# Order of the work inside a turn: VectorE's cosine product, ScalarE's copies and its squares change places in a six-layer attention kernel

## The reference

```
def attn_layer(x, Wqkv, qs, ksc, Wo):
    qkv = x @ Wqkv
    q, k, v = jnp.split(qkv, 3, -1)          # 16 heads of 64
    q = l2norm(q) * qs
    k = l2norm(k) * ksc
    q = q * cos * scale + rotate_half(q) * sin * scale
    k = k * cos * inv + rotate_half(k) * sin * inv
    out = local_attention(q, k, v)           # windows of 32 rows: own window and the one before
    return out @ Wo
...
for i in range(DEPTH):                       # DEPTH = 6
    x = attn_layer(shift_tokens(x), ...) + x
    x = ffn_layer(shift_tokens(x), ...) + x  # layer norm, x @ W1, a * gelu(gate), @ W2
```

## Time and profile before

| | |
|---|---|
| median of 3 runs | 2216.33 us |
| the profiled execution | 2233.99 us, span 2232.2 us |
| TensorE busy | 1985.9 us, 89% |
| VectorE busy | 1626.6 us, 73% |
| GpSimd busy | 1375.4 us, 62% |
| ScalarE busy | 1295.5 us, 58% |
| mean granted TensorE clock | 0.933 of full speed |

### The profile page before, as it was taken

One profiled execution on the slowest core, in us unless ns is written; L12 is line 12 of the kernel. 1 busy time (PEld: TensorE's weight loads), 2 busy tenths in 40 slices (PEclk: granted clock), 3 DMA queues, 4 the chain that ended last, 5 costly groups with the idle time before them and its releaser, 6 DMA issues.

```text
span 2232.2 us, 74626 instructions
## 1 busy us (share of the span) xinstructions
PE 1985.9 (89%) x33032; PEld 1350.5 (61%) x33032; DVE 1626.6 (73%) x1657; ACT 1295.5 (58%) x1547; POOL 1375.4 (62%) x1401
## 2 busy tenths in 40 slices
PE   2678998679999999999999899998999999999986
PEld 1234444357766676666766666666766766676664
DVE  4546564289886888777877788788778976888753
ACT  1145556556765766666566666665666665766642
POOL 1000000399977787679687867787777877887720
PEclk7589999889999999999999899999999999999998
DMA  2410110023332223322223222233222332222221
GB/s 86 122 43 33 33 53 12 26 55 73 71 83 70 64 60 80 82 72 65 57 65 83 74 71 66 69 83 83 60 71 61 78 85 69 68 61 61 63 64 43
DMA packets 132866, 146.28 MB, mean 66 GB/s; under 512 B 60856, under 2 KB 75452, under 8 KB 131776
## 3 DMA queue, kind: packets, MB, share of 16 engines
q1 hardware_dynamic: 132544, 141.51, 25.2%
HBM read 30.51 MB, written 5.44 MB: 16 GB/s over the span
## 4 chain that ended last, share of the span: by engine, by line
DVE 33%; PE 25%; POOL 11%; SPq 10%; issue 9%; ACT 9%; DMA 2%; DVEq 0%; POOLq 0%; ACTq 0%
DVE arena L736 8%; SPq L1266 7%; DVE ss L728 4%; POOL arena L1110 4%; DVE arena L777 4%; DVE arena L767 3%; PE banks L408 3%; DVE mx_t L763 3%; PE banks L575 3%; PE banks L480 3%; DVE arena L639 3%; PE banks L391 2%; POOL arena L1118 2%; ACT arena L995 2%; PE banks L370 2%
## 5 line engine op out<-in xcount | busy, mean ns | idle before, releaser
L1110 POOL TENSOR_TENSOR arena<-arena,tab_sl 128x512 f32<-128x512 f32 x384 | 546.3, 1454 | 37.0 <-ACT arena L931 30.4
L1118 POOL TENSOR_TENSOR arena<-arena 128x1024 f32<-128x1024 f32 x192 | 491.5, 2581 | 0.0
L736 DVE TENSOR_TENSOR arena<-arena,rn 128x1024 f32<-128x1024 f32 x192 | 355.2, 1891 | 79.7 <-POOL rn L1086 79.7
L960 ACT ACTIVATE arena<-arena 128x1024 f32<-128x1024 f32 x96 | 101.5, 1058 | 534.2 <-DVE arena L767 534.2
L471 PE MATMUL banks<-w_qkv,arena 128*128 128x512 f32 x768 | 356.6, 607 | 7.4 <-ACT arena L923 5.5
L538 PE MATMUL banks<-arena 64*64 64x32 f32 x12288 | 252.1, 226 | 42.7 <-DVE arena L767 41.8
L480 PE MATMUL banks<-ident,arena 128*128 128x128 f32 x1536 | 231.7, 307 | 50.2 <-DVE arena L777 32.5
L538 PEld LDWEIGHTS banks<-arena 64*64 64x64 f32 x12288 | 241.0, 139 | 57.4 <-DVE arena L767 48.0
L639 DVE TENSOR_REDUCE arena<-banks 128x1 f32<-128x1024 f32 (+7 forms) x176 | 175.2, 1027 | 124.3 <-PE banks L372 124.1
L880 ACT ACTIVATE arena<-banks 128x1024 f32<-128x1024 f32 (+4 forms) x176 | 150.1, 870 | 153.5 <-PE banks L393 139.3
L480 PEld LDWEIGHTS banks<-ident,arena 128*128 128x128 f32 x1536 | 194.6, 158 | 70.9 <-DVE arena L777 49.8
(11 more groups left out here) (112 smaller groups left out, 3159.2 us busy)
## 6 DMA issues: line engine op xcount, KB each, us to landing
arena<-arena SPq DMA_DIRECT2D x1512, 64.0 KB, 2.0
w_qkv<-Wqkv SPq DMA_DIRECT2D x6, 1024.0 KB, 5.6
arena<-parts_dram SPq DMA_DIRECT2D x96, 48.0 KB
arena<-parts_dram SPq DMA_DIRECT2D x32, 144.0 KB
parts_dram<-arena SPq DMA_DIRECT2D x4, 768.0 KB, 3.3
w_o<-Wo SPq DMA_DIRECT2D x6, 512.0 KB
w_qkv<-Wqkv SPq DMA_DIRECT2D x6, 512.0 KB, 4.2
arena<-X SPq DMA_DIRECT2D x24, 128.0 KB
```

Source lines behind the costliest of these rows:

```text
L736: e.tensor_tensor(to, to, rn[n // 2 % 2][:, n % 2, HEADS * m:HEADS * (m + 1)].unsqueeze(2).to_broadcast([P, HEADS, HEAD_DIM]), ALU.mult).t ...
L1110: e.tensor_tensor(qk_sw[:, m, :].rearrange("p (h d) -> p h d", d=HEAD_DIM)[:, :, d:d + HALF], raw[:, m, :].rearrange("p (h d) -> p h d", d ...
L1118: e.tensor_tensor(to, to, qk_sw[:, m, :], ALU.add).then_inc(S["rs"], 1)
```

## The change

In VectorE's turn `rotate(s)` moves ahead of `norms(s-1)`. In ScalarE's turn `project(s)`, which now only copies, moves ahead of `exponents(s-4)`; the two squares become a function `squares(s)` of their own, between `values(s-2)` and `weights(s-4)`. No instruction is added or removed, and TensorE's, GpSimd's and the DMA queue's programs are the same.

```
 VectorE
                 if 0 <= s - 4 < n_tiles:
                     subtract(s - 4)
+                if s < n_tiles:
+                    rotate(s)
                 if 0 <= s - 1 < n_tiles:
                     norms(s - 1)
-                if s < n_tiles:
-                    rotate(s)
...
 ScalarE
                     e.copy(raw[:, m, :], banks[:, pair_of["proj", n, m], :]).then_inc(S["raw"], 1)
+
+            def squares(n):
+                raw = qk_raw[n % 2]
                 w.wait_ge(S["ss_sum"], n)
...
+                if s < n_tiles:
+                    project(s)
                 if 0 <= s - 4 < n_tiles:
                     exponents(s - 4)
-                if s < n_tiles:
-                    project(s)
...
                 if 0 <= s - 2 < n_tiles:
                     values(s - 2)
+                if s < n_tiles:
+                    squares(s)
                 if 0 <= s - 4 < n_tiles:
                     weights(s - 4)
```

## The result

The change is slower: 2244.36 us against 2216.15 us (medians of 4 runs each), ratio 1.0113, interval 1.0077 to 1.0149 (the two medians alone give 1.0127). A second set of runs of the same change gave 1.0081, 1.0057 to 1.0104. The predicted +0.95% lies between the two ratios. Two sets of one kernel can so differ by 0.3%, and a smaller difference between two kernels says little.

What follows compares the result with a forecast made beforehand. TensorE, 94% busy from 1100 to 2180 us, bounds the kernel through its waits and speed. -4 + 8 + 0 + 21 - 6 + 2 = +21 us: 2233.99 to 2255, or 2237 from the median (+0.95%); range +12 to +32 us, chance 0.48.

Steps and rivals of the forecast that it cites:

- The waits for 777 go and come back at 519: TensorE's 32.5 us of waits at line 480 for cosine products mostly move to line 519, for normalised weights; -4 us.
- a rival: Faster: waits for 777 go for good, slow matmuls could become fewer; -32.5 us, up to 2184, or 2200; chance 0.22.
- Norms later: Sum of squares 2.2 us later delays GpSimd's rn and the subtraction before the k=3 gather; 16 x 0.5 = +8 us.
- The k=3 turn and the squares: Gather to gather from k=3 grows by 1.0 us, through late normalise and squares ahead of the GELUs; 21 groups, +21 us.
- the two chains: In k=3, one over normalise, one over squares and GELUs; both put the next gather 21 us after this one.
- Scale and GpSimd: VectorE's scale runs beside GpSimd's products instead of additions; k=1 gains up to 0.7 us, k=2 can lose it; 0 booked.
- The extra 7 us: If each half of scale in k=1 lost to one GpSimd product, the sum would be about 7 us higher; left out.
- A layer's change: Five times GpSimd waits for the last cosine product before making tables; it comes earlier, half of 2.2 us counted; -6 us.
- Run-in: Turns 4 to 9, without feed-forward: the norms' chain gets longer in three pairs of turns; +2 us, at most +6.6.
- GpSimd in k=0: Later norms stay hidden, since scale stands behind `ff_down`; about 1 us to spare, no cost.
- The signs that I had named: 777 waits near 0, 756 over 60 us, norms 4.5 us behind subtraction, k=3 rn wait 3 us, weights' copy gather + 10.

Runs made afterwards that it cites:

- ScalarE's order alone: The change with VectorE's norms put back ahead of rotate, ScalarE's new order kept; ratio 1.0346 to the kernel before.
- the fastest kernel: The change with squares right behind the exponents and VectorE's sum of squares of the turn's own tile last, behind normalise; 0.9743 of the kernel before, 2165.59 us.

## Why the prediction was right, and where its steps were not

**The waits for 777 go and come back at 519.** Right: none in the list, and 50.6 us more at 519. What I left out is the clock. I booked -4 us for the step and spoke of the slow matmuls only in a rival. The granted clock rose from 0.96 to 0.99, and k=0 got 0.7 us shorter, where I had booked nothing. Put back in two kernels, VectorE's old order costs 0.4% (0.9993 against 0.9955) where ScalarE is late in k=1 alone, and 2.3 to 2.6% (1.0346 against 1.0113 and 1.0081) where it is late in k=3 too.

**Norms later.** The mechanism is as predicted: rn 3.55 us late in k=3 (I had said about 3), the gather then starts with the subtraction. The chain from the subtraction in k=2 to that in k=3 takes 16.5 us, the median over all turns (14.1 before, 16.3 predicted). The term was mis-sized all the same: k=2 is not longer, 15.9 us, where I had booked +0.5. TensorE now starts the k=2 gather itself 1.1 us behind the subtraction (1337.28 against 1336.14), having waited 1.23 us for line 923. With that wait out of the way k=2 grew by 0.4 us. The price is paid in k=3, as loss of the 1.8 us of slack.

**The k=3 turn and the squares.** Right as to place, and the two chains came out as worked out, with line 519 at gather + 7.7 (7.5 predicted) and the subtraction at gather + 21.46 (21.0). The term was mis-sized: +1.6 us in k=3 in place of +1.0. And its share was wrong: I took the chains as equal, so that removing one would gain little, but moving the squares out of the GELUs' way gained 28 to 35 us, since the slack at the next gather shortens k=0 as well.

**Scale and GpSimd.** Booked at 0. The scale of k=1 fell from 4.4 to 3.6 us in the mean, about as far as I had allowed, and that of k=2 did not lose it again (4.8 before, 4.4 after). TensorE gained nothing by it: in k=1 it is held by line 923. The extra 7 us that the prediction set beside its sum did not come either; before the k=1 gather TensorE waits for the subtraction twice, 2.0 us in all.

**A layer's change.** Predicted -6 us; k=2 and k=3 together fell by 2.0 us in each of 5, -10 us, and k=0 gave 0.7 back (17.7 to 18.4). The gather there waits 2.5 us (it was 3.9) and no longer runs slow, 2.52 us in place of 4.29; the transposes behind it still do, 3.62 us:

```profile
1279.50 2.52 PE L538 MATMUL banks<-arena 64*64 64x32 f32 x128 [2.52 <-DVE arena L767]
1281.95 3.62 PE L480 MATMUL banks<-ident,arena 128*128 128x128 f32 x16
```

**Not foreseen:** the copies of line 923 behind the squares, 20.1 us of waits. I had followed the squares only to the weights and the GELUs. In the groups its net price is small or none (1.0066 against 1.0081 and 1.0113).

**Run-in.** Predicted +2 us, at most +6.6. The turns that I meant, 5 to 9, took 5.4 us more, and up to the gather of turn 12 it is 10.2. With the squares of turns 7 and 11 behind line 923 these turns take 115.4 us in place of 121.9, and 115.1 with the squares last everywhere: two thirds of this loss goes with the squares' place ahead of line 923.

**GpSimd in k=0.** Hidden, as predicted: the last step of rn ends at 1384.45 + 0.32 = 1384.77, and scale starts at 1386.12, behind `ff_down`.

The signs that I had named all came: no wait for 777, 68.7 us for 756, norms 4.5 us behind the subtraction, the weights' copy of k=3 at gather + 9.9. But the time came out of a sum in which a gain that was booked too low (the clock) and losses that were booked too low (the squares, the run-in) stood against each other, so that it fits so well is in part luck. Nor can the trace pair settle the sum: its turns account for its 10 us, and the other 18 or so of the 28 are the distance of the profiled execution before from its own median, which no trace places. The sign rests on the squares: with them out of the way the same change is 0.4 to 0.6% faster than before.

## What to carry to other kernels

When work moves earlier on one engine, look at what stands behind both moved pieces: it did not get earlier, and the stall reappears at the first instruction that needs it. A piece that is moved to "near the end of a turn" has to be followed past everything that ends the turn in every kind of turn, here the GELUs in one of four and the copies for the next group in another. The slack at a meeting of two engines is worth as much as a wait: a chain that ends just in time makes the next turn pay. And it can pay to put a sum that nobody needs within the turn (here the sum of squares) last in it, if its operand can be ready there: together with copies first, rotate first and early squares that gave 2.6%, while the same place in VectorE's turn alone, without the copies first, cost 4.2%.

## What the runs showed of the hardware

Short waits of TensorE can cost more than their length, but not each time. The granted clock in these traces is at one of two levels, full (2.4 GHz) or half (1.2 GHz). Two k=2 turns of the kernel before have the same two waits, of 1.17 and 0.96 us:

```profile
739.06 2.52 PE L538 MATMUL banks<-arena 64*64 64x32 f32 x128 [1.17 <-DVE arena L767]
742.55 3.38 PE L480 MATMUL banks<-ident,arena 128*128 128x128 f32 x16 [0.96 <-DVE arena L777]
...
1400.94 2.52 PE L538 MATMUL banks<-arena 64*64 64x32 f32 x128 [1.17 <-DVE arena L767]
1404.43 2.22 PE L480 MATMUL banks<-ident,arena 128*128 128x128 f32 x16 [0.96 <-DVE arena L777]
```

The first time the transposes took 3.38 us, the second time 2.22, with the granted clock of the stretch at 0.81 and at 1.00:

```profile
739.00:748.00 9.00, 7.97 (x151) 6.71 (x152) 7.91 (x9) 7.97 (x10) 5.56 (x15) 0.81 0.13 32
1401.00:1410.00 9.00, 7.84 (x177) 5.83 (x185) 7.91 (x8) 8.97 (x11) 5.68 (x15) 1.00 0.20 48
```

Of 26 turns before the change with a wait at line 538 and another at 480, 14 had transposes of over 3 us; with ScalarE's order alone it was 24 of 35. Single waits can do it too: 7 turns of the change had slow transposes behind one wait of 0.8 to 2.5 us. No turn without a wait at either line had them, in any of these traces. From 560 to 2120 us the clock was at half for 109 us before, for 34 us in the change, although TensorE is idle 35 us more there, and for 167 us with ScalarE's order alone. In the fastest kernel waits of some 3 us in one piece bring it to 116 us. So fewer waits in pairs went with less time at half the clock, and the idle time in sum does not tell it. What decides in the single case, these runs don't show.

A scale of two halves took 2.35 us alone, 3.3 to 4.0 us beside GpSimd's products (about 1.1 us each alone) and 4.5 to 6.7 us beside its additions (2.3 us each). That agrees with the Trainium skill, page "SBUF — State Buffer", section "Who interferes with whom": a VectorE instruction with two SBUF inputs contends with a GpSimd instruction that reads SBUF, and the ports that they share are an exclusive lock. So what a VectorE instruction costs here depends on which GpSimd instruction it meets.
